# A two-layer decoder on one core: the causal attention's keys, half its values and its queries computed inside the norm behind the Mamba block, with that norm in four PSUM banks

## The chip, the cores and the metric

The kernel runs on one NeuronCore of a Trainium2 chip. PE is TensorE (matmuls), DVE is VectorE, ACT is ScalarE, POOL is GpSimd, SP issues the loads. The metric is the device time of one execution in microseconds (us); the median of several executions is compared.

## What is computed

The reference is a decoder of two layers on x (32 sequences of 56 tokens, 128 features), with a layer norm behind every block. The last four steps matter here:

```python
x = _layernorm(x + _L0_ffn_ref(x, ...), axis=-1)
x = _layernorm(x + _L1_attn_ref(x, ...), axis=-1)            # a Mamba block
x = _layernorm(x + _L1_xattn_ref(x, ctx_1024, ...), axis=-1) # causal attention
x = _layernorm(x + _L1_ffn_ref(x, ...), axis=-1)
```

`_L1_xattn_ref` projects queries from x but keys and values from the context, of which the causal mask leaves the first 56 positions:

```python
q = (x @ Wq + bq)                                # 16 heads of 8
kv = context @ Wkv + bkv
att = q @ k.T / sqrt(8), masked causally, softmax
y = (att @ v) @ Wp + bp
```

So the keys and the values depend on no earlier block; the queries need the normed output of the Mamba block.

## The kernel before, in words

The program is a sequence of stages, each made of one or more `nc.Block()`s. In a block every engine has an instruction list of its own, in the order in which the code writes it, and waits on semaphores for the others; at the end of a block all engines meet. There is no scheduler: the order of the code is the order of the queue. The 1,792 tokens are worked on in NC = 4 chunks of CH = 448 (8 sequences each), and a chunk is TPC = 4 tiles of 112 tokens.

Three blocks in a row are concerned.

**The norm `mn`** (`stage_norm`, L267, called at the end of `stage_mamba`, L2367). Per chunk PE adds the residual (L307) and the Mamba output projection (`project`, L2364, two products per tile) into the PSUM tile `y`; DVE takes statistics of it (L331, L335); ACT takes the square root (L383); DVE takes the reciprocal (L347) and writes the normalised tiles to `x_tm` (L356); PE transposes these into a second PSUM tile `xt` (L313); ACT copies `xt` to `core.xT` (L399). `y` and `xt` have four banks each, all eight of PSUM. PE transposes chunk c two steps behind its projection, and DVE's statistics of chunk c stand ahead of its normalising of chunk c-1. POOL and SP have nothing here.

**The preparation block `cq`** (`stage_causal`, from L2456). It has all eight PSUM banks as `ps`. PE makes the keys of four chunks (L2491, k < 4) from `cT`, the context already transposed, then the queries of four chunks from `core.xT` into the same four banks (L2491, k >= 4), each after its bank's keys have been taken out, then the values in four groups of eight sequences (L2498). The keys are stored per head: `kblk[:, b, x, :]` holds the keys with all but every fourth head's rows set to nought, so every chunk of keys is taken out HR = 4 times, each with a mask column `head4` and a bias. DVE does that for three chunks (L2552, 12 instructions), ACT for the fourth (L2521, 4). ACT takes out the queries (L2525). The values go into `vblk`, a block-sparse tile, by two instructions per group on each of DVE (L2555) and ACT (L2529). `vblk` is zeroed ahead, half by DVE (L2533) and half by POOL (L2470); POOL also makes the head mask (L2462 to L2467) and the causal mask (L2472 to L2476). DVE clears the pads of `qT` (L2534), makes `onesb` (L2535, L2539), the columns `head4` and `kbias` (L2541, L2545) and `bv` (L2547), all of it ahead of the keys.

**The pair loop `clp`** (from L2560): 16 pairs of sequences go through scores (PE L2583), mask and maximum (DVE), subtraction (POOL), exponential (ACT), transposes (PE L2594), and products with the values (PE L2608, L2612).

The weights of the causal attention and `cT` are loaded by SP at the start of the scan block of the Mamba stage (`load_causal`, L256), which is long over by the norm.

## Time and profile before

| | us |
|---|---|
| median of 3 executions | 1214.89 (1213.7 to 1215.18) |
| the profiled execution | 1214.09 |
| its span | 1212.4 |
| norm `mn`, first product to last copy | 1038.1 to 1057.3 |
| preparation block `cq` | 1057.6 to 1079.8 |
| pair loop `clp`, from its first product | 1080.06 |

Over the span PE is busy 84%, DVE 81%, ACT 57% and POOL 50%; the granted clock of TensorE is 0.914 of 2.4 GHz in the mean. Times in the rows count from the start of the span. "Granted clock" is 1.00 at 2.4 GHz and 0.50 at 1.2 GHz. A row of the view in order of time gives start and length of an instruction or of a run of like ones, and in square brackets how long the engine had been idle and what ended that. `mn_y`, `mn_xt`, `cq_ps`, `clp_pA` and so on are the tiles named above with their stage ahead of them. A product of 32-bit numbers is two MATMUL rows in the trace.

### The profile page before, as it was taken

Reading aid. Unit: us, or ns where it says so; the run is one execution under the profiler, and the core shown is the slowest. Engines: PE = TensorE matmul, PEld = TensorE weight load, DVE = VectorE, ACT = ScalarE, POOL = GpSimd, SP = SyncE. Lnnn points to the kernel's source line nnn. Section 1 sums busy time; section 2 is a strip of 40 time slices with the busy share of each in tenths; the row PEclk is TensorE's granted clock in tenths of the full one; section 3 lists DMA queues with packets and bytes.
Section 4 is the critical chain, followed back from the end, with each engine's and each line's share of the span. In section 5 each row is a group of like instructions: output and inputs, shape, how many; then the busy total and the mean of one; then the engine's idle time right before and its main releaser. Section 6 shows DMA issues by size and latency. Waiting matters only on the chain. (4 is left out here: it accounts for less than half of the span.)

```text
span 1212.4 us, 22018 instructions
## 1 busy us (share of the span) xinstructions
PE 1015.6 (84%) x8207; PEld 754.4 (62%) x8207; DVE 976.3 (81%) x1855; ACT 685.9 (57%) x1454; POOL 600.7 (50%) x826
## 2 busy tenths in 40 slices
PE   8889998576799999999999798691678778768797
PEld 6556654253799999999998656530233333536655
DVE  5999999756698988988886447777999999577675
ACT  4677674064566666666665163266656655147553
POOL 4500000012888888888884231011999997125360
PEclk9999988788899999999999889796798988869989
DMA  3000000030211112112100010000100000000001
GB/s 76 1 2 1 2 1 1 4 111 25 113 52 69 64 75 77 64 68 77 72 7 1 1 24 2 0 1 25 42 1 1 0 0 1 1 1 3 3 1 31
DMA packets 18763, 33.35 MB, mean 28 GB/s; under 512 B 5200, under 2 KB 13888, under 8 KB 18656
## 3 DMA queue, kind: packets, MB, share of 16 engines
q1 hardware_dynamic: 18144, 31.89, 7.9%
q8 instruction: 65, 1.06, 0.4%
q14 instruction: 42, 0.34, 0.1%
q10 hardware_dynamic: 512, 0.05, 0.0%
HBM read 31.02 MB, written 0.92 MB: 26 GB/s over the span
## 5 line engine op out<-in xcount | busy, mean ns | idle before, releaser
L2274 POOL TENSOR_TENSOR m_h_in<-m_dtu,m_bs 128x896 f32<-128x896 f32 x64 | 132.0, 2091 | 56.9 <-ACT m_bs L2295 56.9
L803 DVE SCALAR_TENSOR_TENSOR l0r_u<-l0r_u,l0r_a_col 128x1024 f32<-128x1024 f32 x110 | 136.3, 1281 | 4.1 <-ACT l0r_u L710 4.0
L1184 POOL TENSOR_TENSOR bl_sc<-bl_sc,bl_topall 125x1456 f32<-125x1456 f32 x32 | 105.3, 3290 | 58.8 <-ACT bl_topall L1346 58.8
L2351 DVE TENSOR_TENSOR_SCAN m_hs<-msp_da,m_h_in 128x896 f32<-128x896 f32 x64 | 129.1, 2019 | 6.0 <-ACT msp_da L2313 5.6
L710 ACT ACTIVATE l0r_u<-l0r_pu 128x512 f32<-128x512 f32 x218 | 109.4, 638 | 32.0 <-PE l0r_pu L610 32.0
L610 PE MATMUL l0r_pu<-l0r_xs,l0r_eb 32*128 32x256 f32 x896 | 110.1, 470 | 5.8 <-ACT l0r_u L710 3.6
L1421 PE MATMUL bl_pS<-b_qw,bl_xcT 128*125 128x112 f32 x768 | 104.0, 278 | 0.0
L610 PEld LDWEIGHTS l0r_pu<-l0r_xs,l0r_eb 32*128 32x128 f32 x896 | 75.9, 214 | 38.7 <-ACT l0r_u L710 27.5
L2233 PE MATMUL msp_py<-m_hc,ident 128*128 128x448 f32 x192 | 93.4, 617 | 3.2 <-DVE m_gT L2342 3.2
L896 POOL MEMSET bq_lT<- 128x256 f32 x1 | 0.3, 311 | 192.8 <-POOLq L528 192.8
L1353 ACT ACTIVATE bl_sq<-bl_pX 125x512 f32<-125x512 f32 x96 | 57.2, 597 | 62.8 <-PE bl_pX L1410 34.5
L1421 PEld LDWEIGHTS bl_pS<-b_qw,bl_xcT 128*125 128x125 f32 x768 | 91.5, 189 | 0.0
L1410 PE MATMUL bl_pX<-b_mk,bl_xcT 128*125 128x128 f32 x768 | 91.2, 276 | 0.0
L1410 PEld LDWEIGHTS bl_pX<-b_mk,bl_xcT 128*125 128x125 f32 x768 | 88.0, 191 | 0.2 <-ACT bl_xcT L1291 0.2
L1261 DVE TENSOR_REDUCE bl_top<-bl_sc 125x112 f32<-125x1456 f32 x32 | 86.3, 2697 | 1.5 <-DVE bl_sc L1241 0.5
L1241 DVE TENSOR_TENSOR bl_sc<-bl_pS,bl_inv 125x448 f32<-125x448 f32 x96 | 59.1, 620 | 27.0 <-PE bl_pS L1421 27.0
L2313 ACT ACTIVATE msp_da<-m_dt,mw_alog 128x440 f32<-128x440 f32 x128 | 75.2, 624 | 2.2 <-DVE m_hs L2351 2.0
L1275 DVE TENSOR_REDUCE bl_ss<-bl_sq 125x8 f32<-125x512 f32 x96 | 62.8, 682 | 13.9 <-ACT bl_sq L1353 9.8
L808 DVE TENSOR_SCALAR l0r_u<-l0r_u 128x1024 f32<-128x1024 f32 x112 | 72.3, 688 | 0.0
L1199 POOL TENSOR_SCALAR b_xc<-b_xc,bl_rstd,bl_shift 125x128 f32<-125x128 f32 x160 | 69.3, 456 | 1.7
L1199 POOL TENSOR_SCALAR bl_more<-bl_more,bl_rstd,bl_shift 125x128 f32<-125x128 f32 x160 | 69.3, 457 | 1.7
L1291 ACT ACTIVATE bl_xcT<-bl_pX 128x500 f32<-128x500 f32 x96 | 52.7, 584 | 19.7 <-PE bl_pX L1393 19.6
(402 smaller groups left out, 2431.0 us busy)
## 6 DMA issues: line engine op xcount, KB each, us to landing
b_xc<-in_ctx SPq DMA_DIRECT2D x16, 750.0 KB
bl_more<-in_ctx SPq DMA_DIRECT2D x16, 750.0 KB
x_tm<-in_x SPq DMA_DIRECT2D x1, 896.0 KB, 8.3
cw_cT<-in_ctx_headT SPq DMA_DIRECT2D x1, 896.0 KB, 4.5
out_dram<-x_tm SPq DMA_DIRECT2D x4, 224.0 KB, 2.5
l0r_xr<-in_x SPq DMA_DIRECT2D x4, 192.0 KB, 4.8
w_up<-in_L_ffn_w SPq DMA_DIRECT2D x1, 512.0 KB, 4.1
w_down<-in_L_ffn_w SPq DMA_DIRECT2D x1, 512.0 KB, 5.3
```

The costliest lines, as they stand in the source:

```text
L610: last = pe.matmul(out, eb[rows, half, j0 + j, :, :], x, start=True, stop=True)
L710: act.activation(u[:, c % RC, :, :, at:at + 2 * B].rearrange("p t r x -> p (t r) x"), pu[:, n % NPU, :].rearrange("p (a x) -> p a x", x=2 ...
L803: ve.scalar_tensor_tensor(state(c, i, r), prev, a_col[:, :], state(c, i, r), ALU.mult, ALU.add).then_inc(s["step"], 1)
L1184: pool.tensor_tensor(sc[0:KP, n % 3, :, :], sc[0:KP, n % 3, :, :], over(topall[0:KP, n % 2, :].unsqueeze(1), [KP, KT + 1, QR]), ALU.subtra ...
L1199: last = pool.tensor_scalar(context(n)[:, t, :], context(n)[:, t, :], rstd[:, b, t:t + 1], shift[:, b, t:t + 1], ALU.mult, ALU.add)
L1261: ve.tensor_reduce(top[0:KP, n % 2, :], sc[0:KP, n % 3, :, :].rearrange("p k q -> p q k"), AX, ALU.max).then_inc(s["top"], 1)
L1410: last = pe.matmul(pX[0:KP, u, r * D:(r + 1) * D], xcT[:, n % 2, at], mk[:, :], start=True, stop=True)
L1421: last = pe.matmul(pS[0:KP, u, r * QR:(r + 1) * QR], xcT[:, n % 2, t * KP:(t + 1) * KP], qw[:, n, :], start=False, stop=(r == KS - 1))
L2233: last = pe.matmul(py[:, half, 0:CH], core.ident[:, :], of[:, half, :], start=(st == 0), stop=(st == DS - 1))
L2274: pool.tensor_tensor(h_in[:, n % NI, :, :], dtu[:, k % 2, :, :], both_halves(bs[:, n % NB, :]), ALU.mult).then_inc(s["db"], 1)
L2313: act.activation(da[:, n % 2, half * CH:(half + 1) * CH].rearrange("p (b t) -> p b t", t=L)[:, :, 1:L], dt[:, half, span(k)].rearrange("p ...
L2351: ve.tensor_tensor_scan(hs[:, n % NS, :, :].rearrange("p h q -> p (h q)"), da[:, n % 2, 0:H2 * CH], h_in[:, n % NI, :, :].rearrange("p h q ...
```

## The change

- `stage_norm` gets `narrow`: `xt` is then `y` itself, each chunk's transposes being written over the bank whose contents have just been normalised. The norm holds four banks instead of eight. ACT's copy to `xT` now signals (`kept`).
- `stage_norm` gets hooks (`beside`) for PE, DVE, ACT and POOL at each step.
- `stage_mamba` no longer runs the norm; it returns `project`, and `gT` (the gated output) lives in a scope that outlasts it. The norm is run by `stage_causal`, with four banks `kv` beside it.
- **PE** in the norm: keys of chunks 0 and 1 behind the projections of chunks 0 and 1, two groups of values behind the first transposes, queries of chunk k behind the transposes of chunk k+1 (the last two together at the end), keys of chunks 2 and 3 behind queries 0 and 1.
- **ACT** in the norm: the keys of three chunks (12 instructions) and the four query evictions, interleaved with the norm's own work. **DVE**: the head mask by a reduction over the identity, `head4`, `kbias` and the pads of `qT` at the start, the keys of the fourth chunk (4 instructions) at the end. **POOL**: all of `vblk` zeroed, the causal mask.
- What stays in the block `cq`: two groups of values on PE, all value copies on DVE and ACT, and on DVE, behind them, `onesb` and `bv`.

The core of the diff:

```diff
-        xt = psum("xt", [P, NC, 512]) if outT else None
+        xt = y if narrow else psum("xt", [P, NC, 512]) if outT else None
+        follow = router is not None or narrow
...
+                    if beside and "tensor" in beside:
+                        beside["tensor"](pe, c, y, kept)
...
+                if beside and "vector" in beside:
+                    beside["vector"](ve, 0)
                 for c in range(NC + 1):
                     if c < NC:
                         statistics(c)
                     if c:
                         normalise(c - 1)
+                if beside and "vector" in beside:
+                    beside["vector"](ve, 1)
...
-                        if router is not None:
+                        if follow:
                             act.activation(to, view(xt[:, c - 2, 0:CH]), ACT.Copy).then_inc(kept.sem, 1)
...
+                    if beside and "scalar" in beside:
+                        beside["scalar"](act, c, y)
...
+                def products(pe, c, y, kept):
+                    def keys(k):
+                        if k == 0:
+                            pe.wait_ge(w.loaded, CAUSAL_LOADED)
+                        if k >= 2:
+                            pe.wait_ge(ktaken, HR * (k - 1))
+                        pe.matmul(kv[:, k % 2, 0:CH], wqkv[:, 1, :], cT[:, k * CH:(k + 1) * CH], start=True,
+                                  stop=True).then_inc(kmade, 1)
+                    def queries(k):
+                        pe.wait_ge(kept.sem, kept(k + 1))
+                        pe.matmul(y[:, k, 0:CH], wqkv[:, 0, :], core.xT[:, k * CH:(k + 1) * CH], start=True,
+                                  stop=True).then_inc(qmade, 1)
+                    if c < 2:
+                        keys(c)
+                    if c == 2:
+                        for g in range(EARLY):
+                            values_made(pe, g, kv[:, 2 + g, :])
+                    if 3 <= c < NC + 3:
+                        queries(c - 3)
+                    if c in (3, 4):
+                        keys(c - 1)
...
+                def evictions(act, c, y):
...
+                    for x in ((0, 1), (2, 3, 4), (5, 6), (7, 8, 9), (10,), (11,))[c]:
+                        keys_taken(act, x)
+                    if c == NC:
+                        query(0)
+                    if c == NC + 1:
+                        query(1)
+                        query(2)
+                        query(3)
...
+                def small(ve, when):
+                    if when == 0:
+                        ve.tensor_reduce(head[:, :], core.ident[:, :].rearrange("p (h e) -> p h e", e=DH1), AX, ALU.add).then_inc(spread, 1)
+                        ve.memset(qT[:, :, L:LP], 0.0)
...
+                    else:
+                        ve.wait_ge(kmade, NC)
+                        for r in range(HR):
+                            to, of = keys_at(NC - 1, r, kv)
+                            ve.tensor_scalar(to, of, bqk[:, 1:2], head4[:, r:r + 1], ALU.add, ALU.mult)
...
+                def fills(pool):
+                    pool.memset(vblk[:, 0:B // 2, :, :], 0.0)
+                    pool.memset(vblk[:, B // 2:B, :, :], 0.0)
...
+                stage_norm(core, "mn", project=gated_projection, doubled=True, outT=by_batch(core.xT), narrow=True,
+                           beside={"tensor": products, "scalar": evictions, "vector": small, "gpsimd": fills})
...
+                with scope(core, "cq") as (_, psum3), nc.Block() as block:
+                    ps = psum3("ps", [P, B // VB - EARLY, 512])
+                    @block.tensor
+                    def _(pe):
+                        for g in range(EARLY, B // VB):
+                            values_made(pe, g, ps[:, g - EARLY, :])
...
+                    @block.vector
+                    def _(ve):
+                        values(ve, lambda o, x: ve.tensor_copy(o, x), 0)
+                        ve.memset(onesb[:, :, :], 0.0).then_inc(zeroed, 1)
```

Three places in the order of the instructions show what moves. Lines are each kernel's own, so the norm's L307, L313, L383 and L399 read L308, L314, L390 and L404 in the changed one.

PE, from the last products of chunk 2 to the first of chunk 3 in the norm, before:

```order
L307 MATMUL mn_y<-x_tm,ident 112x128
L2364 MATMUL mn_y<-mw_wout,m_gT 112x128 x2
L313 MATMUL mn_xt<-ident,x_tm 128x112 x4
L307 MATMUL mn_y<-x_tm,ident 112x128
L2364 MATMUL mn_y<-mw_wout,m_gT 112x128 x2
```

and now:

```order
L308 MATMUL mn_y<-x_tm,ident 112x128
L2374 MATMUL mn_y<-mw_wout,mg_gT 112x128 x2
L314 MATMUL mn_y<-ident,x_tm 128x112 x4
L2478 MATMUL ckv_kv<-cw_wqkv,cw_cT 56x64 x32
L308 MATMUL mn_y<-x_tm,ident 112x128
L2374 MATMUL mn_y<-mw_wout,mg_gT 112x128 x2
```

Behind the transposes of chunk 0 stand now 32 products for the values of groups 0 and 1, ahead of the projection of chunk 3 (the keys of chunks 0 and 1 stand in the same way ahead of the projections of chunks 1 and 2).

PE, the end of the norm and the block behind it, before:

```order
L313 MATMUL mn_xt<-ident,x_tm 128x112 x12
L296 UNCONDITIONAL_BRANCH
L2481 UNCONDITIONAL_BRANCH
L2491 MATMUL cq_ps<-cw_cT,cw_wqkv 128x448 x4
L2491 MATMUL cq_ps<-xT,cw_wqkv 128x448 x4
L2498 MATMUL cq_ps<-cw_wqkv,cw_cT 56x64 x64
```

and now:

```order
L314 MATMUL mn_y<-ident,x_tm 128x112 x4
L2497 MATMUL mn_y<-xT,cw_wqkv 128x448
L2492 MATMUL ckv_kv<-cw_cT,cw_wqkv 128x448
L314 MATMUL mn_y<-ident,x_tm 128x112 x4
L2497 MATMUL mn_y<-xT,cw_wqkv 128x448
L2492 MATMUL ckv_kv<-cw_cT,cw_wqkv 128x448
L314 MATMUL mn_y<-ident,x_tm 128x112 x4
L2497 MATMUL mn_y<-xT,cw_wqkv 128x448 x2
L297 UNCONDITIONAL_BRANCH
L2569 UNCONDITIONAL_BRANCH
L2478 MATMUL cq_ps<-cw_wqkv,cw_cT 56x64 x32
```

The twelve transposes in a row are split; queries and the last keys stand between them, and of the preparation block 32 products for values are left.

ACT, the norm and the start of the preparation block, before:

```order
L371 ACTIVATE mn_warm<-eps_ln 112x1
L383 ACTIVATE mn_std<-mn_mv,eps_ln 112x4 x3
L399 ACTIVATE xT<-mn_xt 128x448
L383 ACTIVATE mn_std<-mn_mv,eps_ln 112x4
L399 ACTIVATE xT<-mn_xt 128x448 x3
L296 UNCONDITIONAL_BRANCH
L2515 UNCONDITIONAL_BRANCH
L2521 ACTIVATE cl_kblk<-cq_ps,cl_kbias,cl_head 128x8x56 x4
L2525 ACTIVATE cl_qT<-cq_ps,cw_bqk 128x8x56 x4
L2529 ACTIVATE cl_vblk<-cq_ps 56x16x2x8 x8
```

and now, from the square root of chunk 2:

```order
L390 ACTIVATE mn_std<-mn_mv,eps_ln 112x4
L404 ACTIVATE xT<-mn_y 128x448
L2517 ACTIVATE cl_kblk<-ckv_kv,cl_kbias,cl_head 128x8x56 x2
L390 ACTIVATE mn_std<-mn_mv,eps_ln 112x4
L404 ACTIVATE xT<-mn_y 128x448
L2517 ACTIVATE cl_kblk<-ckv_kv,cl_kbias,cl_head 128x8x56 x3
L404 ACTIVATE xT<-mn_y 128x448
L2517 ACTIVATE cl_kblk<-ckv_kv,cl_kbias,cl_head 128x8x56
L2523 ACTIVATE cl_qT<-mn_y,cw_bqk 128x8x56
L404 ACTIVATE xT<-mn_y 128x448
L2517 ACTIVATE cl_kblk<-ckv_kv,cl_kbias,cl_head 128x8x56
L2523 ACTIVATE cl_qT<-mn_y,cw_bqk 128x8x56 x3
```

Ahead of the third square root stand five of the keys' instructions; between the last square root and the last query eviction stand 12 instructions in place of three copies.

## Rows read from the trace of the kernel before

**Rows 1.** Stretches of the span: per engine busy us (instructions); granted clock; DMA share, GB/s.

```profile
1038.00:1057.50 19.50, 15.03 (x112) 14.09 (x112) 10.72 (x52) 4.62 (x10) 0.00 (x0) 0.85 0.00 1
1057.50:1080.00 22.50, 16.62 (x144) 8.60 (x144) 15.69 (x31) 7.75 (x16) 5.04 (x8) 0.67 0.01 1
1080.00:1142.00 62.00, 49.55 (x1186) 35.83 (x1187) 39.86 (x57) 41.81 (x84) 31.54 (x17) 0.92 0.01 3
```

**Rows 2.** PE in order of time, last scan products and norm: start, length, line, tiles, [idle before].

```profile
1030.71 4.67 PE L2233 MATMUL msp_py<-m_hc,ident 128*128 128x448 f32 x12
...
1042.45 0.38 PE L307 MATMUL mn_y<-x_tm,ident 112*112 112x128 f32 x2
...
1045.09 0.38 PE L307 MATMUL mn_y<-x_tm,ident 112*112 112x128 f32 x2
...
1048.12 0.60 PE L313 MATMUL mn_xt<-ident,x_tm 112*128 112x112 f32 x4 [0.23 <-DVE x_tm L356]
...
1050.76 0.60 PE L2364 MATMUL mn_y<-mw_wout,m_gT 128*112 128x128 f32 x4
...
1054.22 0.60 PE L313 MATMUL mn_xt<-ident,x_tm 112*128 112x112 f32 x4 [2.48 <-DVE x_tm L356]
...
1055.71 1.01 PE L313 MATMUL mn_xt<-ident,x_tm 112*128 112x112 f32 x4 [0.89 <-DVE x_tm L356]
```

**Rows 3.** DVE in order of time, from the norm's last chunk to the values.

```profile
1051.40 0.89 DVE L331 BATCH_NORM_STATS2 mn_raw<-mn_y 112x6 f32<-112x128 f32 x4 [0.66 <-PE mn_y L2364]
...
1054.29 1.37 DVE L356 TENSOR_SCALAR x_tm<-mn_y,mn_mv,mn_rstd 112x128 f32<-112x128 f32 x4
...
1058.48 3.47 DVE L2533 MEMSET cl_vblk<- 128x4096 f32 x1 [2.82 <-PEq L296]
...
1062.18 0.11 DVE L2535 MEMSET cl_onesb<- 128x64 f32 x1
...
1063.00 0.50 DVE L2547 COPY c_bv<-cw_bv 64x112 f32<-64x112 f32 x2
...
1063.52 7.92 DVE L2552 TENSOR_SCALAR cl_kblk<-cq_ps,cw_bqk,cl_head 128x448 f32<-128x448 f32 x12
...
1076.41 3.35 DVE L2555 COPY cl_vblk<-cq_ps 56x256 f32<-56x256 f32 x8 [4.97 <-PE cq_ps L2498]
```

**Rows 4.** ACT in order of time, the same stretch.

```profile
1052.73 0.30 ACT L383 ACTIVATE mn_std<-mn_mv,eps_ln 112x4 f32<-112x4 f32 x1 [2.70 <-DVE mn_mv L335]
...
1056.75 0.54 ACT L399 ACTIVATE xT<-mn_xt 128x448 f32<-128x448 f32 x1 [1.35 <-PE mn_xt L313]
...
1063.26 2.57 ACT L2521 ACTIVATE cl_kblk<-cq_ps,cl_kbias,cl_head 128x448 f32<-128x448 f32 x4 [5.96 <-DVE cl_kbias L2545]
...
1074.88 0.63 ACT L2525 ACTIVATE cl_qT<-cq_ps,cw_bqk 128x448 f32<-128x448 f32 x1 [0.86 <-PE cq_ps L2491]
```

**Rows 5.** PE in order of time, preparation block and first scores.

```profile
1066.27 1.86 PE L2491 MATMUL cq_ps<-xT,cw_wqkv 128*128 128x448 f32 x2 [3.25 <-DVE cl_kblk L2552]
...
1074.77 4.19 PE L2498 MATMUL cq_ps<-cw_wqkv,cw_cT 128*56 128x64 f32 x128
...
1080.06 0.64 PE L2583 MATMUL clp_pA<-cl_kblk,cl_qT 32*64 32x224 f32 x16 [1.10 <-PEq L2456]
```

**Rows 6.** Short stretches, columns as in rows 1: the clock around the norm.

```profile
1038.00:1041.00 3.00, 2.90 (x14) 2.93 (x15) 0.00 (x0) 1.49 (x2) 0.00 (x0) 0.52 0.00 0
...
1050.00:1054.00 4.00, 1.74 (x17) 1.53 (x15) 3.27 (x16) 0.76 (x3) 0.00 (x0) 1.00 0.00 0
...
1054.00:1057.50 3.50, 1.61 (x8) 1.05 (x8) 1.62 (x6) 1.09 (x2) 0.00 (x0) 0.67 0.00 0
```

**Rows 7.** PE in order of time, score products of three pairs.

```profile
1087.71 1.05 PE L2583 MATMUL clp_pA<-cl_kblk,cl_qT 32*64 32x224 f32 x16
...
1092.84 0.63 PE L2583 MATMUL clp_pA<-cl_kblk,cl_qT 32*64 32x224 f32 x16
...
1107.70 0.64 PE L2583 MATMUL clp_pA<-cl_kblk,cl_qT 32*64 32x224 f32 x16
```

More of the change, by code:

```diff
@@ L267, in stage_norm @@
 def stage_norm(core, name, project=None, doubled=False, rms=False, gain=None, shift=None,
[L268 removed]
+               residual=True, outT=None, beside=None, ready=None, second=False, router=None, narrow=False):
     nc = core.nc
@@ L413, in _ @@
                     beside["sync"](sp)
+            if beside and "gpsimd" in beside:
                 @block.gpsimd
@@ L426, in stage_norm @@
         turned.base += NC if outT else 0
-        kept.base += NC if router is not None else 0
+        kept.base += NC if follow else 0
         logits.base += NC if router is not None else 0
@@ new lines, in keys_at, with values_made @@
+            def keys_at(c, x, kv):
+                return kblk[:, c * BC:(c + 1) * BC, x, :], kv[:, c % 2, 0:CH].rearrange("p (b t) -> p b t", t=L)
+            def values_made(pe, g, to):
+                for r in range(VB):
+                    b = VB * g + r
+                    for i in range(2):
+                        wv = wqkv[:, 2, :].rearrange("f (r i q e) -> f r i q e", r=RG, i=2, q=2)[:, :, i]
+                        last = pe.matmul(to[i * LP:i * LP + L, r * 64:(r + 1) * 64], cT[:, b * L:(b + 1) * L], wv,
+                                         start=True, stop=True)
+                last.then_inc(vmade, 1)
@@ L2502, in values @@
-                def values(eng, copy, i):
-                    rows = slice(i * LP, i * LP + L)
-                    for g in range(B // VB):
-                        eng.wait_ge(pre, 2 * NC + g + 1)
-                        for k in range(2):
-                            src = ps[rows, 4 + g, :].rearrange("p (x k q e) -> p x k q e", k=2, q=2, e=DH1)[:, :, k]
-                            dst = vblk[rows, g * VB:(g + 1) * VB, :, :].rearrange("p b (y k q) c -> p (b y) k q c", k=2, q=2)[:, :, k]
-                            copy(dst[:, :, :, k * 16 + i * DH1:k * 16 + (i + 1) * DH1], src)
@@ new lines, in stage_causal, with values, _ @@
+                stage_norm(core, "mn", project=gated_projection, doubled=True, outT=by_batch(core.xT), narrow=True,
[6 more added lines that the diff above has]
+                            values_made(pe, g, ps[:, g - EARLY, :])
+                    def values(eng, copy, i):
+                        rows = slice(i * LP, i * LP + L)
+                        for g in range(B // VB):
+                            eng.wait_ge(vmade, g + 1)
+                            of = kv[rows, 2 + g, :] if g < EARLY else ps[rows, g - EARLY, :]
+                            for k in range(2):
+                                src = of.rearrange("p (x k q e) -> p x k q e", k=2, q=2, e=DH1)[:, :, k]
+                                dst = vblk[rows, g * VB:(g + 1) * VB, :, :].rearrange("p b (y k q) c -> p (b y) k q c", k=2, q=2)[:, :, k]
+                                copy(dst[:, :, :, k * 16 + i * DH1:k * 16 + (i + 1) * DH1], src)
+                    @block.scalar
+                    def _(act):
+                        values(act, lambda o, x: act.activation(o, x, ACT.Copy), 1)
+                    @block.vector
+                    def _(ve):
+                        values(ve, lambda o, x: ve.tensor_copy(o, x), 0)
+                        ve.memset(onesb[:, :, :], 0.0).then_inc(zeroed, 1)
+                        ve.wait_ge(zeroed, 1)
+                        for i in range(2):
+                            for k in range(2):
+                                ve.memset(onesb[i * LP:i * LP + L, k, k * 16 + i * DH1:k * 16 + (i + 1) * DH1], 1.0)
+                        for i in range(2):
+                            ve.tensor_copy(bv[i * 64:(i + 1) * 64, :], over(bv2[i * 64:(i + 1) * 64, i:i + 1], [64, T2]))
```

134 lines of the change are left out of this document (40 added, 94 removed).

## The prediction

> **What bounds the kernel now.** I read the stretches first. The norm behind the Mamba block and the preparation block of the causal attention take 42 of the 1212 us, and in neither is any engine full: PE works 15.0 of 19.5 us and 16.6 of 22.5 us, at a granted clock of 0.85 and 0.67, DVE 10.7 and 15.7, ACT 4.6 and 7.8, POOL 0 and 5.0 [rows 1]. So both are chains of engines waiting for each other, and what lies on the chain changes. Then I read each engine in order of time. In the norm PE sets the pace up to the end of the last chunk's projection at 1051.36, and had to wait for DVE only 0.23 us before [rows 2]. What follows is a tail of 5.9 us: statistics of the last chunk, square root, two chunks normalised, transposes, copy to 1057.29 [rows 3, 4]. In the preparation block the chain is DVE's: it starts at 1058.48, 0.9 us after the block's beginning at 1057.6, zeroes half of `vblk` (3.47 us), does 1.5 us of small work, and only then, at 1063.52, takes out keys for 7.9 us [rows 3]. The queries' products wait for the banks that these keys hold (3.25 us before the first) and run at half clock, 1.86 us for the two passes of one product [rows 5]. Then come the values on PE and the copies on DVE up to 1079.76, and the first scores at 1080.06 [rows 3, 5]. None of the keys' and values' work needs the norm, so what can run beside it can leave the chain.
>
> **The change, part by part.** The instruction order shows that the work does move. Times are those of the profiled execution.
>
> *PE in the norm.* Ahead of the end of the last projection stand now two products for keys and 32 for values. A full-clock product of this width costs 4.67 us / 6 = 0.78 us by the scan's last ones [rows 2]. All 64 value products were 128 passes in 4.19 us, 32 of them thus 2.1 us; the first quarter of these took 1.6 us, until DVE's copy began at 1076.41, and the other 96 passes 2.5 us or 0.027 us each, so 64 passes cost 1.7 us at full clock and 3.2 at half [rows 3, 5]. The granted clock was 1.00 over 1050 to 1054, and PE is busier now, so I take the full clock: 1.5 + 1.7 - 0.23 (the wait, now covered) = **+3.0 us**, and the last projection ends at 1054.4. Taken at half clock, the keys at 1.5 us each and the values at 3.2, it would be +6.0. What rows show of the clock: 0.52 in the norm's first 3 us, and 0.67 in the norm's last 3.5 us, after a stretch in which PE worked 1.7 of 4 us [rows 6]. Of this the Trainium skill, page "TensorE: Matmul & The Clock Gate", section on the HAM clock gate, says that the throttled state is the default and sustained activity releases it. By that rule the denser PE would keep 2.4 GHz in the tail too, which is the +3.0 us; priced at the tail's own rows, at half clock, it is +6.0.
>
> *The tail of the norm.* From 1054.4: statistics 1.3, square root 0.25, done at 1055.95 [rows 3, 4]. Now ACT is the bound: two copies to `xT`, four keys, one query, one more copy, one key and three queries stand behind the square root in its queue (three copies, five keys, four queries in all). A copy is 0.53 us, a key 2.57 / 4 = 0.64, a query 0.63 [rows 4]: 1.6 + 3.2 + 2.5 = 7.3 us, done at 1063.3. I followed who waits for it: DVE normalises chunks 2 and 3 until 57.2 and 58.75; PE has transposes, a query and a key behind each and 6 us of work in 9, so its results come just ahead of ACT's need; DVE takes the last keys, four of 0.66 us, from 59.9 to 62.5. The five keys ahead of the third square root end before the statistics they would delay. The norm block ends at 1063.3 instead of 1057.3: **+6.0 us**, the +3.0 within it. Two bounds: were ACT never kept waiting and its keys all early, the old tail plus one query (0.8 + 0.6 us) gives +4.4; with the tail at half clock (products 1.86 us, transposes 1.0 us [rows 2, 5]) PE becomes its bound: from 57.2, two sets of transposes, three queries and a key are 2 x 1.0 + 4 x 1.86 = 9.4 us, and with the last eviction it ends at 67.3, so +10.
>
> *The preparation block.* It was 22.8 us from 1057.3 to 1080.06. What is left: the meeting of the engines 0.3 us (1079.76 to 1080.06), the eight copies of values 3.35 us on DVE, `onesb` 0.4 us (1062.18 to 1062.57), `bv` 0.5 us, and the meeting again 0.3 [rows 3, 5]. DVE also began its old block 0.9 us after PE; nothing in the trace says why. Between 0 and 0.9 I take 0.9, since it is the same engine at the same boundary. The two groups of values on PE, 1.7 us at full clock, hide behind DVE's first four copies (1.66 us); at half clock the second group comes at +3.2 us and adds 0.7. Sum 0.3 + 0.9 + 3.35 + 0.4 + 0.5 + 0.3 = 5.8 us: **-17.0 us**. All products of queries, the half of the values, 16 evictions of keys, 3.47 us of memset and the wait for banks are gone from the chain.
>
> *POOL* zeroes now all of `vblk`: its old 5.0 us with the half that it had, and 3.5 us (DVE's memset) for the other, 8.5 us in all [rows 1, 3]. It was idle in the norm, so it is done by 1047, 16 us before the first copy needs it. DVE's own work at the start (two reductions, a memset, 1 us) falls into the 4.4 us in which PE makes the first chunk (its next begins at 1042.45 [rows 2]). The loads are long in place. Cost nought; uncovered, DVE's piece would be 1 us.
>
> *What follows.* The pair loop starts behind 3 us in which PE is idle instead of 1.1, so it may begin at half clock: two score products, each 1.05 instead of 0.64 us [rows 5, 7], and a little more: **+0.4 us**, between 0 and 4. (The upper end is two more pairs at the slow pace: 5.1 us from 1087.71 to 1092.84 against 14.86 / 5 = 3.0 us over the next five pairs to 1107.70 [rows 7].) A gain is possible as well if the clock rises sooner than before (between 1087.71 and 1092.84 [rows 7]); bounded by the same two pairs, I allow 2 us.
>
> *Sum:* +6.0 - 17.0 + 0.4 = -10.6 us. Against the profiled execution's 1214.1 that is 1203.5 us. The median of before is 0.8 above its profiled execution, so the median could come out at 1204.3; since the low single values lie at 1213.7, I keep 1203.5.
>
> **Rivals.**
> - *The tail at half clock.* For it: the clock fell at just this point before [rows 6], and PE has gaps behind each transpose still. Against it: by the tracing above PE works two thirds of this stretch, against two fifths in the 4 us before the clock fell [rows 6]. The norm's end moves by 10 instead of 6 us: a gain of about 6.6, **1207.5 us**.
> - *PE at half clock for the whole merged norm.* Before, it was at half clock only for the first 3 us of it: a chunk would take 24 x 2.90 / 14 = 5.0 us instead of 2.64 [rows 2, 6], so three chunks +7.1, and the tail +4 as above: 10.6 - 11.1 gives **about 1214.6**, no change. Little speaks for it.
> - *Slower: the pair loop stays at half clock.* The loop was still slow at 1087.71 before, 7.7 us after its start, and each slow pair costs 5.1 - 3.0 = 2.1 us more [rows 7]. If the longer idle time of PE ahead of it held the clock down through the loop, the sixth additional slow pair would use up the 11.0 us gained; ten of them cost 21: **1224 us**. Against it: a slow loop keeps PE nearly full, and that has brought the clock back within 13 us before.
> - *The queues block each other.* ACT's keys wait for `kbias` and stand ahead of the square roots. If the interleaving stretched the chunks (each late square root delays DVE's normalising, then PE), half of the ACT work of the keys, 4 us, would come back onto the chain: **1207.5 us** as well. My tracing above says ACT has 3 us idle before the last square root, so it would have to be a wait I overlooked.
>
> **How the numbers follow.** A difference of 0.2%, 2.4 us, is about what can be told from none. Forecast (gain 8.5 to 13): 0.72. Tail at half clock or queues blocking (gain 4 to 8): 0.21. About no change: 0.03. The slow loop: 0.02. A larger gain, over 13 us, if DVE's 0.9 us falls away and the clock is better afterwards: 0.02. The range: from 1200.5 (0.9 less for the late start, 2 for the clock, rounded) to 1208.0 (the tail at half clock). Faster 0.95, same 0.03, slower 0.02.
>
> **What would show it.** In the changed profile: the last projection of the norm ends 16.3 us after its first product (13.3 before); ACT without idle time of note from the last square root to the last query eviction, some 7.3 us; the norm block 25.2 us long; the preparation block under 6 us with DVE's eight copies first in it; first scores some 11 us earlier, about 1069. The keys' and queries' products should read 0.54 us a pass and not 0.95. It would be wrong if products in the norm's last 9 us show the long times, if the clock in the pair loop rises much later or sooner after its start than 13 us, or if ACT waits for PE in the tail. Stages from the norm behind the pair loop on should be unchanged in length, within 1 us.

## The result, and the profile after

The changed kernel took 1197.76 us in the median of 4 executions (1194.79 to 1200.37) against 1214.49 for the one before (4 executions): ratio 0.9862, 95% interval 0.9837 to 0.9887. It is faster than the 1203.5 us forecast, and lies under the low end of the range (1200.5). The comparison was made twice more, each time among runs of the same chip: 0.9888 (0.9872 to 0.9905) and 0.9882 (0.9850 to 0.9913). Over the three, 15 executions of the changed kernel have a median of 1198.6 us. Its profiled execution took 1198.54 us, its span 1196.5.

The gain lies where it was expected. From the norm's first product to the first score product it took 1080.06 - 1038.10 = 41.96 us before and takes 1064.17 - 1037.07 = 27.10 us now: 14.86 of the 15.55 us between the two profiled executions. Another 1.0 us is the norm's own start, which came that much earlier. The pair loop, from its first score product to the next norm's first product, took 58.4 us before and now, and what follows it 73.9 in both.

The two stretches in the changed kernel, columns as in rows 1:

```profile
1037.00:1060.00 23.00, 20.85 (x192) 16.70 (x192) 16.33 (x60) 13.88 (x26) 7.94 (x6) 1.00 0.01 2
1060.00:1064.20 4.20, 2.03 (x68) 1.95 (x70) 3.45 (x15) 2.54 (x9) 0.00 (x0) 1.00 0.00 0
```

PE is busy 20.9 of 23 us in the norm, against 15.0 of 19.5 before [rows 1], at a granted clock of 1.00 instead of 0.85; the block behind it is 4.2 us instead of 22.5.

PE in order of time, changed kernel (start, length, line, tiles, count, idle before):

```profile
1037.07 0.44 PE L308 MATMUL mn_y<-x_tm,ident 112*112 112x128 f32 x2 [2.71 <-PEq L2204]
...
1039.77 0.92 PE L2492 MATMUL ckv_kv<-cw_cT,cw_wqkv 128*128 128x448 f32 x2
...
1047.03 2.00 PE L2478 MATMUL ckv_kv<-cw_wqkv,cw_cT 128*56 128x64 f32 x64
...
1051.25 0.60 PE L2374 MATMUL mn_y<-mw_wout,mg_gT 128*112 128x128 f32 x4
...
1054.72 0.60 PE L314 MATMUL mn_y<-ident,x_tm 112*128 112x112 f32 x4 [0.96 <-DVE x_tm L359]
...
1057.06 1.82 PE L2497 MATMUL mn_y<-xT,cw_wqkv 128*128 128x448 f32 x4
...
1060.30 2.00 PE L2478 MATMUL cq_ps<-cw_wqkv,cw_cT 128*56 128x64 f32 x64 [1.41 <-PEq L297]
...
1064.17 0.64 PE L2625 MATMUL clp_pA<-cl_kblk,cl_qT 32*64 32x224 f32 x16 [1.88 <-PEq L2566]
```

The last projection ends at 1051.85, 14.8 us after the first product (16.3 forecast, 13.3 before [rows 2]). Keys are two passes in 0.92 us, and the next product starts 0.75 us after them, close to the 0.78 priced; the values of two groups read 2.00 us (1.93 to the next start), where 1.7 was priced. No pass of a query or key in the tail shows the 0.95 us of half clock [rows 5].

ACT, changed kernel:

```profile
1053.23 0.30 ACT L390 ACTIVATE mn_std<-mn_mv,eps_ln 112x4 f32<-112x4 f32 x1 [3.18 <-DVE mn_mv L338]
...
1053.86 1.95 ACT L2517 ACTIVATE cl_kblk<-ckv_kv,cl_kbias,cl_head 128x448 f32<-128x448 f32 x3
...
1058.31 1.69 ACT L2523 ACTIVATE cl_qT<-mn_y,cw_bqk 128x448 f32<-128x448 f32 x3
...
1060.27 1.20 ACT L2586 ACTIVATE cl_vblk<-ckv_kv 56x256 f32<-56x256 f32 x4 [0.27 <-PEq L297]
```

ACT goes without a gap from the last square root at 1053.23 to 1060.00, as forecast, but needs 6.5 us for its 12 instructions behind it and not 7.3: the three queries in a row are 1.69 us, 0.56 each, where [rows 4] gave 0.63 for one that stands alone.

DVE, changed kernel:

```profile
1037.76 2.80 DVE L2544 TENSOR_SCALAR cl_kbias<-cl_head,cw_bqk 128x4 f32<-128x4 f32 x1
...
1060.29 1.41 DVE L2590 COPY cl_vblk<-ckv_kv 56x256 f32<-56x256 f32 x4 [0.72 <-PEq L297]
...
1061.63 1.45 DVE L2590 COPY cl_vblk<-cq_ps 56x256 f32<-56x256 f32 x4
...
1063.43 0.44 DVE L2597 COPY c_bv<-cw_bv 64x112 f32<-64x112 f32 x2
```

The block behind the norm begins at 1060.29 on DVE, together with PE and ACT. The eight copies take 2.79 us, not 3.35: those of [rows 3] had waited for PE between groups. And one row stands out: `kbias`, an instruction on four elements per partition, reads 2.80 us (0.36 before). Its record ends at 1040.56, but the statistics behind it start at 1039.97, 2.9 us after the norm's first product, as in the narrow norm without it, so it delayed nothing here.

The clock around the norm in the changed kernel, columns as in rows 1:

```profile
1034.00:1037.00 3.00, 0.36 (x1) 0.00 (x0) 2.34 (x3) 0.00 (x0) 1.13 (x1) 1.00 0.00 0
...
1037.00:1040.00 3.00, 2.93 (x25) 2.92 (x26) 2.82 (x5) 1.49 (x2) 2.97 (x1) 1.00 0.00 0
...
1054.00:1057.00 3.00, 2.28 (x12) 1.50 (x13) 2.24 (x9) 3.00 (x6) 0.00 (x0) 1.00 0.03 8
...
1057.00:1060.00 3.00, 1.88 (x7) 0.56 (x5) 2.58 (x4) 3.00 (x6) 0.00 (x0) 1.00 0.00 0
```

PE is idle 2.7 us ahead of the norm, as before, but the granted clock stays at 1.00 through its first 3 us, where before it was 0.52 [rows 6]. The tail, too, stays at 1.00.

### The profile page after: what moved, and what is told of

The parts are those of the page before. It is cut to its first block and busy times, and to the rows that moved or that the text cites. A ratio compares the mean times of both kernels' runs of the same rounds, so it can differ in the third digit from the quotient of the medians.

```text
span 1196.5 us, 22014 instructions
## 1 busy us (share of the span) xinstructions
PE 1003.1 (84%) x8207; PEld 748.8 (63%) x8207; DVE 969.8 (81%) x1847; ACT 689.9 (58%) x1462; POOL 603.3 (50%) x824
## 5 line engine op out<-in xcount | busy, mean ns | idle before, releaser
L620 PE MATMUL l0r_pu<-l0r_xs,l0r_eb 32*128 32x256 f32 x896 | 108.7, 469 | 6.2 <-ACT l0r_u L720 4.0
L620 PEld LDWEIGHTS l0r_pu<-l0r_xs,l0r_eb 32*128 32x128 f32 x896 | 75.5, 213 | 38.1 <-ACT l0r_u L720 27.1
```

The source lines that it names most:

```text
L620: last = pe.matmul(out, eb[rows, half, j0 + j, :, :], x, start=True, stop=True)
```

## The experiments

For each profile the table gives one stretch, from the norm's first product to the first scores. It comes in two sorts: the norm's first four tiles are started 2.7 us or 4.35 us ahead of what follows, as the clock stands at 2.4 or 1.2 GHz in its first 3 us. The table takes those 1.65 us off where the clock was low.

| kernel | clock at the norm's start | stretch, us | at full clock | change from before |
|---|---|---|---|---|
| before | half | 41.96 | 40.3 | |
| narrow norm alone | full | 40.55 | 40.55 | +0.2 |
| changed | full | 27.10 | 27.1 | -13.2 |
| changed, second profile | full | 27.09 | 27.1 | -13.2 |
| changed, third profile | half | 28.76 | 27.1 | -13.2 |
| changed, no values in the norm | half | 28.43 | 26.8 | -13.5 |
| changed, queries back | full | 31.18 | 31.2 | -9.1 |
| changed, keys back | full | 33.97 | 34.0 | -6.3 |
| before, fills moved | half | 38.82 | 37.2 | -3.1 |
| before, POOL made to wait | full | 43.80 | 43.8 | +3.5 |
| before, two memsets exchanged | half | 41.96 | 40.3 | 0.0 |
| merged | half | 25.58 | 23.9 | -16.4 |
| merged, second profile | full | 23.92 | 23.9 | -16.4 |

**Is it the change that brings the clock?** The changed kernel was run again, and once more later.

> The changed kernel once more, for more executions and a second profile. Theory A (the work taken off the chain is worth more than I priced: the three stages from the norm's first product to the first scores take 27 us instead of 42): the median lies 15 to 17 us under the kernel before, and the norm's first chunk on PE takes 2.7 us or 4.4 us as the clock happens to stand there. Theory B (the change itself brings the full clock at the norm's start): the first chunk takes 2.7 us again, granted clock 1.00 from the norm's first product on.

1199.66 us (5 executions), ratio 0.9888; stretch 27.09 us, full clock at the start. The medians differ by 12.8 us, not by the 15 to 17 expected. The third time:

> The changed kernel beside the merged one on the same chip. Theory A (at like clocks the stretch from the norm's first product to the first scores is 13.2 us shorter; the remainder of the differences seen is the scatter of the stages ahead): 13 us faster than before, within 2 us; the stretch 27.1 us, or 28.8 where the norm starts at half clock; the pair loop 58.4 us again. Rival (the first comparison's 16.7 us holds, some 3 us come from elsewhere in the program): 16 us or more again.

1199.56 us, ratio 0.9882. In its profile the norm starts at half clock; two stretches of 3 us, the one before the norm and its first:

```profile
1038.70:1041.70 3.00, 0.29 (x1) 0.03 (x1) 2.34 (x4) 0.04 (x1) 1.17 (x2) 1.00 0.00 0
...
1041.70:1044.70 3.00, 3.00 (x14) 3.00 (x15) 2.89 (x4) 1.45 (x2) 3.00 (x1) 0.50 0.00 0
```

So the same program meets both clocks. Of the 13 profiles, 6 started the norm at half clock (the kernel before and one variant of it, four with the preparation or part of it moved) and 7 at full clock. Theory B, that the change brings the clock at the norm's start, has fallen. In every one of them PE had been busy until 2.7 us before and was idle from there. The rival that some 3 us come from elsewhere in the program was not confirmed either: both later comparisons are back at 0.988. The start of the norm itself lies anywhere from 1030.6 to 1041.7 us in these profiles, for kernels that are the same up to there, so the whole's difference of two single profiles is good to some microseconds only, while the stretch repeats to 0.02 us at like clock. What moves that start is in part the clock of the stages ahead: in the two of these profiles that start it at 1033.8 and 1041.7 us, 6.0 of the 7.9 us stand already at the first layer's norm (237.6 and 243.6 us), and the 896 products of the first layer's recurrence (L620, the same code in both) read 441 and 476 ns in the mean, at a granted clock of 0.88 and 0.85 over the first 237 us.

The clock at the norm's *end* is another matter. In all five profiles with the old tail (before, narrow norm, fills moved, POOL made to wait, memsets exchanged) PE is idle for 2.48 us and then for 0.5 to 0.9 us between the transposes, and the granted clock falls to 0.50 there. In all six with keys and queries in the tail (the changed kernel three times, the one without early values, the merged one twice) PE's longest wait ahead of the last queries is 0.96 us or none, and the clock stays at 1.00. This part of the clock the change does bring.

**The four banks alone.** The kernel before with only this changed:

```diff
-        xt = psum("xt", [P, NC, 512]) if outT else None
+        xt = y if narrow else psum("xt", [P, NC, 512]) if outT else None
```

> The kernel before with only the norm narrowed to four PSUM banks, everything else where it was. Theory A: no wait arises from the shared bank, so the time is the one before, within 1.5 us, norm block 19.2 us (17.5 if the clock is full at its start), preparation block 22.8 us. Theory B allows either. A rival, that the four banks by themselves save or cost something, would show as more than 2 us.

1211.40 us (12 executions), ratio 0.9996 (0.9982 to 1.0010): no difference. The banks cost nothing and gain nothing by themselves.

**The values.** `EARLY = 0` in place of 2.

> The changed kernel with no group of values in the norm, all four in the block behind it. Theory A: the last projection of the norm ends 2.0 us sooner and the norm with it (21.0 instead of 22.9 us), the block behind takes 2.0 us more (6.2 instead of 4.2 us, PE the bound), so the sum is within 0.7 us of the changed kernel. A rival (what was saved in the preparation block was PE time): 2 us slower.

1200.11 us, ratio 0.9896 (0.9882 to 0.9911), beside 0.9888 for the changed kernel on the same chip: no difference that can be told. At like clock the stretch is 0.3 us shorter. PE in the block behind the norm:

```profile
1060.64 3.79 PE L2478 MATMUL cq_ps<-cw_wqkv,cw_cT 128*56 128x64 f32 x128 [1.41 <-PEq L297]
...
1066.31 0.64 PE L2625 MATMUL clp_pA<-cl_kblk,cl_qT 32*64 32x224 f32 x16 [1.88 <-PEq L2566]
```

Its 128 passes take 3.79 us, and the first scores come 5.7 us after their start; with half of them in the norm it was 3.9 us. The other 2 us stand in the norm, ahead of the last projection. So this part of the change moves work from one place on the chain to another.

**The queries.** Products and evictions back behind the norm:

```diff
-                    if 3 <= c < NC + 3:
-                        queries(c - 3)
...
                     def _(pe):
+                        for k in range(NC):
+                            pe.matmul(qs[k], wqkv[:, 0, :], core.xT[:, k * CH:(k + 1) * CH], start=True,
+                                      stop=True).then_inc(qmade, 1)
                         for g in range(EARLY, B // VB):
```

> The changed kernel with the four queries' products and evictions back in the block behind the norm. Theory A: the norm ends about 1.0 to 1.5 us sooner (ACT has four evictions less in its tail), the block behind takes 3.0 us more (PE 3.0 us of queries ahead of 2.0 us of values), so 1.5 to 2 us slower than the changed kernel, still 13 us faster than before. If the queries by themselves were the large part of the gain, it would be 5 us or more slower.

1203.02 us, ratio 0.9927 (0.9912 to 0.9941). The stretch is 4.1 us longer, not 1.5 to 2. PE:

```profile
1057.37 0.60 PE L314 MATMUL mn_y<-ident,x_tm 112*128 112x112 f32 x4 [1.71 <-DVE x_tm L359]
...
1058.85 0.81 PE L314 MATMUL mn_y<-ident,x_tm 112*128 112x112 f32 x4
...
1061.78 3.32 PE L2565 MATMUL cq_ps<-xT,cw_wqkv 128*128 128x448 f32 x4 [2.12 <-PEq L297]
...
1064.90 2.19 PE L2565 MATMUL ckv_kv<-xT,cw_wqkv 128*128 128x448 f32 x4
```

and the five microseconds around the norm's end, columns as in rows 1:

```profile
1057.70:1062.70 5.00, 2.77 (x11) 1.32 (x10) 4.70 (x11) 2.97 (x6) 0.00 (x0) 0.64 0.00 0
```

Without the queries PE waits 1.71 us for the normalising of chunk 2, its transposes of the last chunk read 0.81 us, and the granted clock falls: the first four passes of the queries take 3.32 us and the next four 2.19, where four took 1.82 us in the changed kernel: 1.9 us more. Here is the rival "tail at half clock" of the prediction, not in the changed kernel but in one that leaves its tail thinner. That gaps in the products' stream bring the throttle back is what the Trainium skill says (page "TensorE: Matmul & The Clock Gate", "HAM oscillation — how this bites in real kernels"), and the tails counted above agree (0.50 in five of five old ones, 1.00 in six of six new ones). But it does not decide this case. The kernel with the keys taken out instead (below) has the same gap and, from the values to the start of the last transposes, products of the same shapes at the same distances, to 0.02 us over 9 us. Its clock stays up (the window lies as the one above does, counted from the last transposes):

```profile
1053.32 0.60 PE L314 MATMUL mn_y<-ident,x_tm 112*128 112x112 f32 x4 [1.71 <-DVE x_tm L359]
...
1054.81 0.60 PE L314 MATMUL mn_y<-ident,x_tm 112*128 112x112 f32 x4
```

```profile
1053.66:1058.66 5.00, 3.92 (x15) 1.73 (x14) 1.09 (x4) 3.30 (x6) 0.00 (x0) 1.00 0.00 0
```

In the kernel without queries the granted clock is 0.50 from 1059.15 on, 0.3 us after the start of its last transposes; up to that start PE had done products of the same shapes at the same distances in both kernels. So a tail with a gap of 1.71 us fell in one profile and not in another. The queries are worth some 2.2 us by their place, and in this profile 1.9 us more by a clock that one profile cannot lay to them. The medians (1203.02 and 1199.66) differ by 3.4 us.

**The keys.** Keys back behind the norm, 12 evictions on DVE and 4 on ACT:

```diff
-                    if c < 2:
-                        keys(c)
...
-                    if c in (3, 4):
-                        keys(c - 1)
...
                     def _(pe):
+                        for k in range(NC):
+                            pe.matmul(ks[k], wqkv[:, 1, :], cT[:, k * CH:(k + 1) * CH], start=True,
+                                      stop=True).then_inc(kmade, 1)
```

> The changed kernel with the keys alone back in the block behind the norm (four products, 12 evictions on DVE and 4 on ACT), queries and two groups of values still in the norm. Theory A (each part is worth what it took of the old chain): the norm is 2 us shorter, the block behind it gets DVE's 7.9 us of keys and some 0.5 us until the first are made, so from the norm's first product to the first scores 33 us instead of 27.1, and the whole 6 us slower than the changed kernel. Rival (the gain came from the fills and queries): within 2 us of the changed kernel.

1206.30 us, ratio 0.9929 (0.9902 to 0.9957); the stretch 33.97 us, 6.9 longer than the changed kernel's (6 expected). DVE:

```profile
1059.06 5.30 DVE L2596 TENSOR_SCALAR cl_kblk<-cq_ps,cw_bqk,cl_head 128x448 f32<-128x448 f32 x8 [4.31 <-PE cq_ps L2566]
...
1064.29 2.69 DVE L2596 TENSOR_SCALAR cl_kblk<-ckv_kv,cw_bqk,cl_head 128x448 f32<-128x448 f32 x4
```

Its keys take 7.9 us in the open, from 1059.06 to 1066.98, as in [rows 3], and copies follow at once. Of the parts undone one by one, the keys are the largest.

**The fills.** The kernel before, with zeroing, masks, `onesb`, `bv` and the columns for the keys in the narrowed norm and nothing else:

```diff
+                stage_norm(core, "mn", project=gated_projection, doubled=True, outT=by_batch(core.xT), narrow=True,
+                           beside={"vector": small, "gpsimd": fills})
```

> The kernel before with its zeroing, masks and small tiles alone moved into the narrowed norm; keys, queries and values stay behind it in their old order (values into banks of their own). Theory A: DVE starts on the keys 5.0 us sooner, at the first product's end, and nothing else changes: the stretch is 36.9 us where the norm starts at half clock (35.3 at full clock) instead of 41.9, so about 5 us faster than before. Rival: the keys' products of PE take the place of the fills as the bound, and half of it is lost, 2 to 3 us faster.

1209.10 us, ratio 0.9956 (0.9930 to 0.9981), 4.9 us faster in the medians (2.3 to 8.5 by the interval). The stretch shows 3.1 us. The block behind the norm gave back 4.4 of the 5.0 us expected: first scores 18.4 us after the last copy to `xT`, 22.8 before. But the norm got 1.3 us longer. DVE, POOL and PE at its start and end:

```profile
1037.23 2.80 DVE L2494 TENSOR_SCALAR cl_kbias<-cl_head,cw_bqk 128x4 f32<-128x4 f32 x1
...
1040.32 3.45 DVE L2501 COPY c_bv<-cw_bv 64x112 f32<-64x112 f32 x2
...
1043.78 0.89 DVE L334 BATCH_NORM_STATS2 mn_raw<-mn_y 112x6 f32<-112x128 f32 x4
```

```profile
1036.49 3.51 POOL L2504 MEMSET cl_vblk<- 128x4096 f32 x1 [0.74 <-SPq L297]
...
1039.94 3.53 POOL L2505 MEMSET cl_vblk<- 128x4096 f32 x1
```

```profile
1047.80 0.60 PE L314 MATMUL mn_y<-ident,x_tm 112*128 112x112 f32 x4 [1.47 <-DVE x_tm L359]
...
1057.28 4.81 PE L2531 MATMUL cq_ps<-cw_cT,cw_wqkv 128*128 128x448 f32 x8 [0.89 <-PEq L297]
```

The copy of `bv`, 0.50 us in [rows 3], reads 3.45 us: it starts behind POOL's second memset of `vblk` and ends 0.3 us behind it. `kbias` likewise ends when POOL's first memset does. The statistics of chunk 0 start at 1043.78, 2.9 us after PE has gone on to chunk 1 (1040.88), 2.7 us later than in the kernel before counted from the norm's first product; from chunk 1 on DVE's norm is late by 1.3 us, and PE waits 1.47 us for the first normalised chunk instead of 0.23. That is a term the prediction did not have: it priced DVE's small work at 1 us at most. The Trainium skill has it (page "SBUF — State Buffer", "Who interferes with whom": VectorE and GpSimd share a pair of ports as an exclusive lock, and a copy or scalar operation of VectorE within SBUF may need it); the trace agrees, with 3.45 for 0.50 us. The change itself leaves `bv` behind the norm, and its `kbias`, at 2.80 us, ends before it is waited for.

**Who is late at the block's start?** DVE began the preparation block 0.9 us behind PE, and the prediction carried these 0.9 us over. POOL was made to wait for DVE's first memset:

```diff
+                    pool.wait_ge(zeroed, 1)
                     pool.memset(head[:, :], 1.0).then_inc(built, 1)
```

> The kernel before with POOL waiting in the preparation block for DVE's first memset. In two profiles DVE began that block 0.9 us behind PE. Theory P (DVE's memset waits for POOL's first small instructions, which end 0.25 us before it starts): it starts now with the block, 0 to 0.3 us behind PE. Theory D (it is DVE's own start of a block): 0.9 us late again. The whole is some microseconds slower either way, since the head mask comes 3.5 us later.

1208.91 us in its one execution, stretch 43.8 us. The stretch is 3.5 us longer than before at like clock, as expected; the whole came out 5 us shorter than the median before and not longer, with a norm that started at 1030.6 us, the earliest of all profiles. With POOL silent, DVE's memset starts at 1049.34, PE's first key at 1048.45: 0.89 us late again. Theory P has fallen. DVE and POOL:

```profile
1049.34 3.47 DVE L2534 MEMSET cl_vblk<- 128x4096 f32 x1 [2.80 <-PEq L296]
...
1053.85 3.27 DVE L2546 TENSOR_SCALAR cl_kbias<-cl_head,cw_bqk 128x4 f32<-128x4 f32 x1
...
1053.98 3.41 DVE L2548 COPY c_bv<-cw_bv 64x112 f32<-64x112 f32 x2
...
1057.41 7.92 DVE L2553 TENSOR_SCALAR cl_kblk<-cq_ps,cw_bqk,cl_head 128x448 f32<-128x448 f32 x12
```

```profile
1053.58 3.51 POOL L2471 MEMSET cl_vblk<- 128x4096 f32 x1
```

These rows also show the lock from the other side: `kbias` (0.36 us in the kernel before) takes 3.27 and ends with POOL's memset at 1057.1; the copy of `bv` ends 0.3 us later, and the keys, whose products had been there for long, start only then. Last, DVE's two first memsets exchanged, the small one first:

```diff
-                    ve.memset(vblk[:, 0:B // 2, :, :], 0.0).then_inc(zeroed, 1)
                     ve.memset(qT[:, :, L:LP], 0.0)
+                    ve.memset(vblk[:, 0:B // 2, :, :], 0.0).then_inc(zeroed, 1)
```

> The kernel before with DVE's first two memsets of the preparation block exchanged, the small one (0.27 us) first. If the 0.9 us by which DVE starts that block late belongs to the large memset, the small one starts with the block and the gap stands before the large one; if it is DVE's entry into this block, the small one is 0.9 us late. The whole is unchanged in both cases.

```profile
1057.03 0.27 DVE L2533 MEMSET cl_qT<- 128x256 f32 x1 [2.02 <-PEq L296]
...
1058.10 3.47 DVE L2534 MEMSET cl_vblk<- 128x4096 f32 x1 [0.80 <-issue]
```

1213.46 us in its one execution. The small memset starts 0.09 us after PE's first product (1056.94), and the gap of 0.80 us stands before the large one. So the 0.9 us belong to DVE's large memset, which reads 3.47 us but costs 4.3; the change gives it to POOL, where it lies beside the norm. What the 0.8 us are isn't shown.

**A version that beats both.** The experiments say that the values' place matters little, that ACT idles 3.18 us before its last square root while five keys wait in the tail, and that the block behind the norm costs 4.2 us mostly for itself. So: keys in four banks and taken out as early as possible (three chunks by ACT before its last square root, one by DVE), values in the same banks once these are free, `onesb` and `bv` in a gap of DVE after POOL's memsets have ended, and no block behind the norm.

```diff
-                    if c < 2:
-                        keys(c)
-                    if c == 2:
-                        for g in range(EARLY):
-                            values_made(pe, g, kv[:, 2 + g, :])
-                    if 3 <= c < NC + 3:
-                        queries(c - 3)
-                    if c in (3, 4):
-                        keys(c - 1)
+                    if c < 3:
+                        keys(c)
+                    if c == 3:
+                        queries(0)
+                        keys(3)
+                        group(0)
+                    if c == 4:
+                        queries(1)
+                        group(1)
+                    if c == 5:
+                        queries(2)
+                        queries(3)
+                        group(2)
+                        group(3)
```

(`group(g)` makes the values of group g into bank g after that bank's keys are out.)

> All of the preparation in the norm, no block behind it: keys in four banks of their own as early as their products come, three chunks taken out by ACT in its idle time before the last square root, the fourth by DVE; the values in the same banks once the keys are out. Theory A: PE becomes the bound, 10.6 us of projections, 2.0 of transposes, 3.0 of keys, 3.0 of queries, 4.0 of values, 22.7 us in all, with the last copies 0.7 and 0.3 us to the first scores: 23.7 us instead of 27.1, 3.4 us faster than the changed kernel (1.7 us more where the norm starts at half clock). Rival (the clock falls in a gap of the tail, or ACT's evictions in the tail stay the bound): 27 us or more, no gain.

1198.47 us, ratio 0.9862 (0.9835 to 0.9889), stretch 25.58 us with a start at half clock. ACT:

```profile
1045.60 2.55 ACT L2537 ACTIVATE cl_kblk<-ckv_kv,cl_kbias,cl_head 128x448 f32<-128x448 f32 x4
...
1052.81 2.56 ACT L2537 ACTIVATE cl_kblk<-ckv_kv,cl_kbias,cl_head 128x448 f32<-128x448 f32 x4
...
1055.97 0.30 ACT L390 ACTIVATE mn_std<-mn_mv,eps_ln 112x4 f32<-112x4 f32 x1 [0.60 <-DVE mn_mv L338]
```

ACT's three times four keys lie ahead of its last square root. Beside the changed kernel on one chip:

> The merged kernel again, to compare with the changed one in the same call. Theory A: the stretch is 23.8 us at full clock or 25.5 where the norm starts at half clock, and the whole 3.2 us faster than the changed kernel, 16 us faster than the one before. Rival: what the merging gains in the stretch is lost behind it, no difference to the changed kernel.

1189.00 us against 1199.56, ratio to before 0.9819 (0.9787 to 0.9852) against 0.9882. PE, second profile of the merged kernel:

```profile
1033.78 0.44 PE L308 MATMUL mn_y<-x_tm,ident 112*112 112x128 f32 x2 [2.71 <-PEq L2204]
...
1052.86 1.82 PE L2496 MATMUL mn_y<-xT,cw_wqkv 128*128 128x448 f32 x4
...
1054.61 2.00 PE L2473 MATMUL ckv_kv<-cw_wqkv,cw_cT 128*56 128x64 f32 x64
...
1057.70 0.64 PE L2639 MATMUL clp_pA<-cl_kblk,cl_qT 32*64 32x224 f32 x16 [1.10 <-PEq L297]
```

PE is at work from 1033.78 to 1056.61 but for 0.2 us, 22.8 us (22.7 worked out), and the scores follow 1.1 us after. The stretch is 23.92 us, 3.2 less than the changed kernel's, as expected. The medians differ by more, 10.6 us, and by 25.2 us from the kernel before, where 16 were expected; the stretch accounts for 3.2 of the 10.6. The rest goes with the clock of the whole execution: the mean granted clock was 0.912 to 0.916 in five of the merged kernel's six executions (0.909 in the slowest, 1198.03 us) and 0.903 to 0.910 in the changed kernel's six, and the two profiles start the norm at 1033.8 and 1041.7 us, the pair compared above. The instructions ahead of the norm are the same, so nothing ties this clock to the merging; why these executions met it is not shown. That the merged kernel is faster is shown by the stretch in two profiles; how much faster in the whole, only roughly.

## Why the prediction was wrong, point by point

*What bounds the kernel* was read rightly: a chain through two blocks with no engine full. Undoing the parts one by one gives 6.9 us for the keys, 4.1 for the queries (1.9 of them a clock that may be that profile's own), -0.3 for the values and, done alone, 3.1 for the fills (4.4 with what they cost in the norm set aside). These need not add up to 13.2, since each is worth what the others leave open.

*The sum for the stretch* was -11.0 us before the pair loop's term. Measured in the pair of profiles: -14.9, at like clock -13.2, which by itself would have come out inside the range, near its low end (1200.9 us). The medians moved by 16.7 us, 6.1 more than the 10.6 forecast: 3.9 of it stand in the stretch, 0.4 is the pair loop's term that did not come, 1.0 is the earlier start of the norm, and 0.8 lies between the profiled executions and the medians. Term by term:

- *PE in the norm*, +3.0 expected. Measured +1.5 in the pair of profiles (14.8 against 13.3), and +3.2 with the 1.65 us of the start taken into account. The products were priced nearly right (3.2 for 3.0: the values cost 1.9 and not 1.7 us). **This is the first failed step**: the clock of the norm's first 3 us, 0.52, stood in [rows 6], and I took it as a property of the kernel. It is one of two states that the same program meets, and it happened to be the low one in the profile of before and the high one in that of after: 1.65 us of the 3.9 by which the stretch beat the sum.
- *The tail*: ACT was the bound, as said. The whole norm +5.4 us at like clock instead of +6.0; 0.6 to 0.8 us from the evictions' pace in a row, 0.56 and 0.61 us instead of 0.63 and 0.64. The half-clock tail did not occur: in the changed kernel the granted clock is 1.00 in the tail in each stretch shown, and in all six profiles with this tail.
- *The preparation block*, -17.0 expected, -18.6 measured (4.17 us left, 5.8 expected). **The second failed step**: 0.9 us of late start carried over "since it is the same engine at the same boundary". The exchange of the two memsets shows that it was the large memset's, and this is one of the instructions that the change takes off DVE. Another 0.56 us: copies priced by a row of eight (3.35 us) that had PE's pace in it, and cost 2.79 back to back.
- *POOL* at nought: right for the change, but by its layout, not by my reason. I had only counted whether POOL's time fits. DVE's small work, put at 1 us, lasted 3.5 us with `kbias` held up, and was covered all the same. The fills alone show what its memsets do to DVE's copies within SBUF: 2.7 us late and 1.3 us on the chain.
- *The pair loop*, +0.4 expected: 58.4 before, 58.4, 58.4 and 58.2 in the three profiles of the changed kernel. Nothing. The term did not add up either: two products at 1.05 for 0.64 us are 0.8 us, not 0.4.

*The rivals.* A slower loop did not come. "Queues block each other" fell: ACT waits 3.18 us before its last square root, as the tracing had it. The larger gain, to which I gave 0.02, is what was measured in the first comparison. Of its two conditions one came, the 0.9 us that fell away; the clock was better at the norm's start and in its tail, not behind. *The range* went wrong on its low side: it had 0.9 us for the late start and 2 for the clock in the pair loop, but nothing for my having priced instructions in a row by those that wait, and nothing for the scatter of the stages ahead, which moved a median of four to six executions by 2 us (the three comparisons: 1197.8, 1199.7 and 1199.6).

## What to carry to other kernels

Price an instruction in a dense queue by rows that did not wait; a run of like instructions timed from first start to last end has its producer's pace in it. Before a gap at an engine's start is carried over to the new code, ask which instruction it stands before, since it may go with that instruction. Filling a norm's idle slots with independent products can pay twice where its tail is thin, by the work and by the clock, but one profile at either clock does not price the second. And keep VectorE's copies within SBUF away from GpSimd's memsets.

## What the runs showed of the hardware

- The granted clock after 2.7 us without a product stays at 2.4 GHz in some executions and is at 1.2 GHz in others of the same program (7 and 6 of 13 profiles of kernels with the same code up to there), for the next 3 us: 1.65 us of 4.35 here.
- In the norm's tail, waits of TensorE of 2.48 and 0.5 to 0.9 us brought 1.2 GHz in five profiles of five, waits of at most 0.96 us left 2.4 GHz in six of six, and one of 1.71 us did either, once each, behind the same 9 us of products.
- GpSimd's memset of 128 x 4096 (3.51 us) held up a VectorE copy of 64 x 112 within SBUF for its whole length (3.45 us for the pair of copies instead of 0.50), and a scalar operation on four elements (2.80 and 3.27 us instead of 0.36). The records of VectorE overlap: behind the held-up scalar operation the statistics started 0.6 us before its record's end. VectorE's own large memset beside GpSimd's was not held up (3.47 us in either case), nor were its readings of PSUM: the statistics of chunk 0 start at 1039.97 in the changed kernel, while GpSimd's first memset is still running.
- In four profiles of the kernel before and its variants VectorE's memset of 128 x 4096 is preceded by 0.8 us in which the engine shows nothing, whether it is the first instruction of its block or the second; a memset of 128 x 256 is not.
